# Decays of two half states of a selective scan made a step early into SBUF, with the softplus logarithm at the start of a step

## The reference

```
u     = silu(conv(x_s));  x_dbc = u @ x_proj_w.T        # gives dt_raw, B, C
delta = softplus(dt_raw @ dt_proj_w.T + dt_proj_b)      # softplus needs exp and log
dA    = exp(delta * A)                                  # one decay per channel, state and position
dBu   = delta * u * B
h[t]  = dA[t] * h[t-1] + dBu[t]                         # for each of 16 states
y[t]  = sum over states of h[t] * C[t];  y += u * D;  y *= silu(z);  out = y @ out_proj_w.T
```

## Time and profile before

| what | value |
|---|---|
| median of 3 runs | 633.02 us (633.02 to 634.33) |
| the profiled execution | 634.19 us, its span 632.4 us |
| DVE busy | 591.2 us, 93% |
| PE, POOL, ACT busy | 545.9, 509.4 and 457.4 us |
| one whole batch, 239.20 to 313.40 us | 74.20 us; DVE 72.39, POOL 69.29, PE 66.78, ACT 57.43 busy |
| table loads on ACT | 1283 ns each; 7 before the logarithm, 5 before an Exp of line 514 |

### The profile page before, as it was taken

One profiled execution on the slowest core, in us unless ns is written; L12 is line 12 of the kernel. 1 busy time (PEld: TensorE's weight loads), 2 busy tenths in 40 slices (PEclk: granted clock), 3 DMA queues, 4 the chain that ended last, 5 costly groups with the idle time before them and its releaser, 6 DMA issues.

```text
span 632.4 us, 11492 instructions
## 1 busy us (share of the span) xinstructions
PE 545.9 (86%) x3560; PEld 427.7 (68%) x3560; DVE 591.2 (93%) x852; ACT 457.4 (72%) x916; POOL 509.4 (81%) x481
## 2 busy tenths in 40 slices
PE   5969988888899998989899898998989697878887
PEld 2368765655877777777687677777777465656564
DVE  6967989999989998999989999899989999899997
ACT  1784899127877698667976688776986579969881
POOL 5795039638999989998999989999898978875783
PEclk9867979979999999999999999999999999899999
DMA  7320106834668788778878788678894345332473
GB/s 221 131 101 0 46 27 127 288 129 158 217 220 262 264 292 252 258 246 266 291 263 270 232 278 285 228 267 269 299 265 157 136 157 216 121 122 80 117 138 84
DMA packets 60894, 122.99 MB, mean 194 GB/s; under 512 B 8219, under 2 KB 41379, under 8 KB 53795
## 3 DMA queue, kind: packets, MB, share of 16 engines
q1 hardware_dynamic: 53826, 112.42, 52.3%
q0 software_dynamic: 6288, 9.52, 7.1%
q10 hardware_dynamic: 720, 0.33, 0.3%
HBM read 112.77 MB, written 9.47 MB: 193 GB/s over the span
## 4 chain that ended last, share of the span: by engine, by line
PE 43%; DVE 21%; ACT 18%; issue 15%; DMA 2%; POOL 0%; DVEq 0%; ACTq 0%
DVE bank L1128 8%; PE bank L1413 8%; PE bank L1562 7%; PE bank L1445 7%; DVE h_sb L1145 6%; PE bank L1576 5%; PE bank L1570 4%; ACT dbu L530 3%; ACT bank L514 2%; PE bank L1468 2%; ACT da L502 2%; PE bank L1460 2%; PE bank L1543 1%; PE bank L1376 1%; DVE lo_oh L1087 1%
## 5 line engine op out<-in xcount | busy, mean ns | idle before, releaser
L915 POOL TENSOR_TENSOR dbu<-du,xn_all 128x512 f32<-128x512 f32 x172 | 215.4, 1275 | 26.8 <-DVE bank L1128 26.4
L1128 DVE TENSOR_TENSOR_SCAN bank<-bank,dbu 128x512 f32<-128x512 f32 x170 | 207.2, 1221 | 9.0 <-ACT bank L514 8.9
L1145 DVE TENSOR_TENSOR h_sb<-bank,xh_all 128x512 f32<-128x512 f32 x240 | 159.3, 678 | 1.2
L514 ACT ACTIVATE bank<-delta,a_sb 128x512 f32<-128x512 f32 x170 | 116.8, 689 | 54.2 <-DVE h_sb L1145 53.5
L1413 PE MATMUL bank<-id_sb,h_sb 128*128 128x128 f32 x992 | 134.8, 281 | 15.2 <-DVE h_sb L1145 13.6
L1413 PEld LDWEIGHTS bank<-id_sb,h_sb 128*128 128x128 f32 x992 | 115.3, 145 | 26.8 <-DVE h_sb L1145 20.4
L1128 DVE TENSOR_TENSOR_SCAN bank<-da,bank 128x512 f32<-128x512 f32 x82 | 96.7, 1214 | 17.1 <-PE bank L1376 17.0
L1562 PEld LDWEIGHTS bank<-wd_sb,hid 117*128 117x128 f32 (+1 forms) x432 | 55.1, 190 | 57.8 <-DVE hid L1179 33.1
L1562 PE MATMUL bank<-wd_sb,hid 117*128 117x128 f32 (+1 forms) x432 | 63.7, 283 | 28.3 <-ACT xT L687 26.7
L902 POOL DMA_INDIRECT xs<-xn_rows,src x72 | 70.7, 981 | 12.4 <-issue 9.1
L530 ACT ACTIVATE dbu<-du_t,bc_sb 128x256 f32<-128x256 f32 x164 | 69.4, 496 | 4.5 <-DVE bank L1128 2.9
(11 more groups left out here) (197 smaller groups left out, 902.9 us busy)
## 6 DMA issues: line engine op xcount, KB each, us to landing
xh_all<-b_rows SPq DMA_DIRECT2D x30, 1024.0 KB, 7.2
xn_all<-b_rows SPq DMA_DIRECT2D x25, 1024.0 KB, 7.2
wgu_sb<-in_w_gu SPq DMA_DIRECT2D x72, 352.0 KB, 2.9
wd_sb<-in_w_dn SPq DMA_DIRECT2D x72, 192.0 KB, 3.3
y_slots<-ys SPq DMA_DIRECT2D x72, 64.0 KB
xn_rows<-xn_all SPq DMA_DIRECT2D x2, 1040.0 KB, 9.9
out<-x_sb SPq DMA_DIRECT2D x7, 256.0 KB, 6.8
x_sb<-in_x SPq DMA_DIRECT2D x2, 640.0 KB, 5.7
```

Of the source, the lines that this page charges most:

```text
L514: nc.scalar.activation(bank_of(b, m)[:, :], delta[b % 2][:, hf, :], ACT.Exp, scale=a_sb[:, hf, k:k + 1]).then_inc(s["da_rdy"], 1)
L915: nc.gpsimd.tensor_tensor(dbu[k % 2][:, hf, :], du[b % 2][:, hf, :], b_ring[c % 2][:, k % CH, :], ALU.mult).then_inc(s["dbu_p"], 1)
L1128: nc.vector.tensor_tensor_scan(at, da_of(n)[:, hf, :] if n in IN_SBUF else at, inp, 0.0, ALU.mult, ALU.add).then_inc(s["h_rdy"], 1)
L1145: nc.vector.tensor_tensor(h_sb[k % 2][:, hf, :], bank_of(b, 2 * k + hf)[:, :], row, ALU.mult).then_inc(s["p_rdy"], 1)
```

## The change

ScalarE makes two decays in step 7 that it made in step 8: half 1 of step 8 and half 0 of step 9. As the PSUM banks are not free then, they go into the SBUF buffer `da[0]`. Step 8 of ScalarE now begins with the logarithm. The two scans that use these decays read them from `da[0]`, and wait themselves until the bank that they write is free. On TensorE, `skip` moves from the end of step 8 to between `gate` and `slots_turn`.

```diff
+        def aside(n, hf):
+
+            b, k = n // S, n % S
+            return 0 < b < NB - 2 and (k, hf) in ((LOG_AT[b], 1), (LOG_AT[b] + 1, 0))
...
+            def decay_aside(n, hf):
+
+                b, k = n // S, n % S
+                nc.scalar.activation(da[0][:, hf, :], delta[b % 2][:, hf, :], ACT.Exp,
+                                     scale=a_sb[:, hf, k:k + 1]).then_inc(s["da_rdy"], 1)
...
-                if b < 6:
+                if b < 6 and k == LOG_AT[b]:
+                    logarithm(b + 1)
+                elif b < 6:
                     decay_bank(g, 1)
...
-                if b < 6:
+                if b < 6 and k != LOG_AT[b]:
                     decay_bank(g + 1, 0)
+                    if k + 1 == LOG_AT[b]:
+                        decay_aside(g + 1, 1)
...
                 if nn is not None:
                     slots_out(nn)
+                if b < 6 and k + 1 == LOG_AT[b]:
+                    decay_aside(g + 2, 0)
...
-                if k == LOG_AT[b]:
+                if b == 6 and k == LOG_AT[b]:
                     logarithm(b + 1)
...
-                nc.vector.tensor_tensor_scan(at, da_of(n)[:, hf, :] if n in IN_SBUF else at, inp, 0.0,
+                if aside(n, hf):
+                    dve.wait_ge(s["p_rdy"], freed(b, 2 * k + hf))
+                    held = da[0][:, hf, :]
+                else:
+                    held = da_of(n)[:, hf, :] if n in IN_SBUF else at
+                nc.vector.tensor_tensor_scan(at, held, inp, 0.0,
                                              ALU.mult, ALU.add).then_inc(s["h_rdy"], 1)
...
                 if nxt is not None:
                     gate(nxt)
+                if 0 < b < NB - 2 and k == LOG_AT[b]:
+                    skip(b)
                 if nn is not None:
                     slots_turn(nn)
...
-                if 0 < b < NB - 2 and k == LOG_AT[b]:
-                    skip(b)
```

## The result

The changed kernel took 645.83 us (median of 4 runs, 644.25 to 646.23), the kernel before 633.02 in the same job. The ratio is 1.020, with a 95% interval of 1.017 to 1.023: **slower, by 12.8 us**. That lies inside the range (632.0 to 649.0), but nearer to rival 1 (648.5) than to the forecast (639.7). The profiled run took 644.25 us with a span of 642.4; the span before was 632.4.

A forecast was written before the change was run, and what follows sets the result against it. VectorE was taken to bound the kernel (72.39 of 74.20 us busy). Losses of 2.1 us (batches 2 to 4), 1.1 (batch 1) and 3.5 (batch 5) summed to 6.7 us slower, 639.7 us; range 632.0 to 649.0.

The forecast's parts named there:

- rival 1: Second new scan loses the port too: 3.0 us in each of four batches, 3.5 in batch 5; 648.5 us; chance 0.22.
- the forecast: First new scan waits 1.40 us, second beats GpSimd's correction, GpSimd falls 2.0 us late: 6.7 us slower, 639.7; chance 0.35.
- VectorE sets the pace, and the gap of 1.81 us goes: VectorE, busy 72.39 of 74.20 us, loses its wait before step 9's scan in five batches: 9.05 us if nothing else late.
- Without the port, 5.8 us: Gain if port conflicts cost nothing: 0.88 us in batch 1 plus 1.23 in each of four others.
- Both limits that I named: TensorE's chain to step 11 allows 1.23 us a batch; GpSimd's slack at step 0 is 1.32, or 0.88 from batch 1.
- The place of the copy: With skip ahead of the turn, ScalarE's copy around step 8 can begin at 250.48, not 251.44: TensorE 0.96 us earlier.
- Two SBUF inputs against GpSimd: Two scans a batch, both inputs in SBUF, contend with GpSimd for the port: between nothing and several us a batch.
- 0.15 is nearest to the first, so I take it that the scan wins: Step 8: GpSimd's correction leads the second scan by 0.15 us; scan runs at 250.68, correction ends 253.1 instead of 251.08.
- Batch 5, 3.5 us: No gather: first scan starts after products and correction at 472.51; second, due 474.69, waits until 477.4, where it was 473.91.
- rival 2: VectorE and GpSimd take the port instruction by instruction in turn; GpSimd ends 1.8 us late: 1.1 slower, 634.1; chance 0.2.

The follow-up runs named there:

- experiment 1: Changed kernel, but each new scan reads one input from PSUM (old bank content, min for mult) instead of two from SBUF: 627.73 us, ratio 0.993.
- experiment 7: Kernel of experiment 1 with TensorE's skip back behind the turn: 626.32 us, ratio 0.991.
- experiment 3: Against the kernel before: only half 0 of step 9 made early into SBUF, in step 8 ahead of the logarithm, skip ahead of the turn: 643.05 us, ratio 1.017.
- experiment 4: Kernel of experiment 3, with GpSimd waiting for the early-decay scan ahead of its correction (batch 5: behind it): 629.40 us, ratio 0.9965.
- experiment 2: Kernel before, order unchanged, one decay moved to SBUF: step 8, half 1, 633.55 us, ratio 1.002; step 9, half 0, 647.95 us, ratio 1.023.

## Why the prediction was right, and where it was not

- **VectorE sets the pace, and the gap of 1.81 us goes.** Right: its wait of 8.9 us for ScalarE is 0.0 after, and VectorE is busy without a break in batch 2.
- **Without the port, 5.8 us.** The size was right. From first scan to first scan, batches 1 to 5 of experiment 1 are 0.77, 1.23, 0.97, 1.29 and 1.40 us shorter than before, 5.7 in all, where I had 0.88 and four times 1.23. The median fell by 4.4 (interval 3.4 to 5.8). Both limits that I named show: a wait of 0.29 us for `dbu` where batch 2 begins, and one of 0.21 for TensorE ahead of the unit of step 11. The place of the copy was right too: 3.38 us behind the scan of step 8, half 1, by my sum, and 3.27 to 3.44 in the trace, where it was 4.34. The reason that I gave was wrong: the new place of the skip is not what brings the copy forward. With the skip behind the turn again, in experiment 7, it comes earlier still (2.84), and batches 1 to 5 are 0.80, 1.21, 1.21, 1.32 and 1.89 us shorter, 6.4 in all, close to GpSimd's slack of 0.88 and 1.32 in the first four.
- **Two SBUF inputs against GpSimd.** Right, and the whole cost: experiment 1 keeps the order and the number of instructions and takes one SBUF input away, and the cost is gone. Also right in detail are the first scan (2.65 to 2.67 in batches 2 to 4, forecast 1.22 + 1.40) and the gather (1.71, ending 0.77 behind the scan, forecast 0.78).
- **The step that failed: "0.15 is nearest to the first, so I take it that the scan wins".** GpSimd's lead was 0.18 us in batch 2 and the scan lost, in all four batches. With it fell the way in which the time was to be lost. The forecast had the second scan at about 1.3 us, GpSimd's correction held up by it, and new waits for `dbu` in steps 14, 15 and 0. The changed profile has the scan at 4.64, the correction still at 1.28, and no wait for `dbu`: the whole loss stands in the scans, as rival 1 had it. I had read the earlier trace rows as a threshold of lead between 0.06 and 0.62 us. There is none: a scan has lost where GpSimd led by 0.14, and has lost where it started 0.54 ahead of the operation that then held it up. The earlier trace rows held the answer (two products back to back, no turn between them), and I used it for the first scan and not for the second.
- **The earlier trace rows are of another kind.** Their GpSimd operations are TENSOR_SCALAR of 128x128, and not 128x512 products. The changed kernel has the same place in batch 0:

```profile
35.58 1.41 DVE L1150 TENSOR_TENSOR_SCAN bank<-da,dbu 128x512 f32<-128x512 f32 x1 [0.35 <-ACT da L507]
36.24 2.31 POOL L844 TENSOR_SCALAR xn_all<-x_sb,mean,both 128x128 f32<-128x128 f32 x1
```

The GpSimd operation before, of 0.79 us, began at 35.46, ahead of the scan, and the next one was ready behind it; the scan got in between the two all the same, and the next one waited for it and for the second scan. Whether it is their shape, their length or their single large input that lets the scan in, no run here tells.
- **Batch 5, 3.5 us: a term sized wrong,** it was 1.0. The first scan was to start at the end of the row of three operations, and started inside it (3.90); the second was to wait for a new row of three, and got in after one (1.47), since that row began with a wait.
- **Instruction by instruction in turn (rival 2).** The rule of the Trainium skill (SBUF — State Buffer, "Who interferes with whom"), that who starts first holds the port for one instruction, gave 634.1 us. The traces disagree in 55 places of 58. They agree where GpSimd had just waited, and beside the TENSOR_SCALAR operations of batch 0.

So the sign came out as forecast because both the forecast's case and rival 1 lie on the slower side, and the time is inside the range because its upper end was rival 1's. The mechanism of batches 1 to 4 is rival 1's and not the forecast's: its four terms of 3.0 measured 3.4, 3.3, 3.3 and 3.0, and its 3.5 was 2.5 too large. In the two profiled executions batches 0 and 6 take the 14.0 down to a difference of 10.1; why the medians differ by 12.8 and not by 14.0 is not settled.

## What to carry to other kernels

Before a VectorE operation with both inputs in SBUF goes next to GpSimd products of 128x512, count those that stand back to back from its start, for it may wait for all of them; the wait shows as a longer operation, and not as idle time. If it must stand there, have GpSimd wait on the semaphore of that operation, where GpSimd has slack: 0.8 us of pause a batch turned 10.9 us slower (experiment 3) into 2.6 us faster (experiment 4). And a loss placed just in front of an existing wait is nearly free (experiment 2), so a change that removes a wait takes that cover from everything ahead of it.

## What the runs showed of the hardware that I had not expected

- A waiting VectorE scan does not get in between 128x512 operations of GpSimd that are issued back to back, though it does between 128x128 TENSOR_SCALAR ones (1.41 us): it took 2.7, 3.9 and up to 5.4 us for 1.2 us of work, with one, two or three more operations behind the running one.
- It gets in ahead of an indirect gather (0.16 us of issue stands before it), which is then 1.7 us long, not 0.98; but a scan that starts 0.46 us into a gather loses to the operation that is ready behind it, and one that starts 0.10 into it does not.
- Where GpSimd's first operation had waited for a semaphore, the scan gets in before the second (1.47 to 1.50 us, the second 2.19). A memset of 0.12 us before or between does not do it. By what means the wait matters is open; the traces show only when.
